# Graph attention and graph convolution on one core: products of 258 columns, the ones of the adjacency counted in the second layer, products ordered mask by mask, and a reordered first stage

## The reference

```python
h = jnp.maximum(_layernorm(x, axis=-1), 0.0)
# layer 0: graph attention, then a gated update
Wh = h @ W
src = Wh @ a[:F_out];  dst = Wh @ a[F_out:]
e = jax.nn.leaky_relu(src + dst.T, 0.2)
att = softmax(jnp.where(adj > 0, e, NEG_INF), axis=1)
h_prime = att @ Wh
gi = h_prime @ w_ih.T + b_ih;  gh = h @ w_hh.T + b_hh      # r, z, n as in a GRU cell
x = x + ((1.0 - z) * n + z * h)
# layer 1: graph convolution
h = jnp.maximum(_layernorm(x, axis=-1), 0.0)
x = x + adj @ (h @ W1.T + b1)
```

## Time and profile before

| | |
|---|---|
| median of 3 runs | 1602.78 us (1601.82 to 1603.23) |
| the profiled execution | 1601.98 us, of which the span is 1600.4 us |
| PE busy | 1534.7 us, 96% of the span |
| DVE busy | 1125.8 us, 70% |
| ACT busy | 1071.0 us, 67% |
| POOL busy | 40.5 us, 3% |
| DMA | 454.15 MB, mean 284 GB/s |

### The profile page before, as it was taken

The page is one execution under the profiler, slowest core; times in us unless marked ns, Lnnn a source line. Parts: engine busy times, 40 slices in busy tenths (PEclk is TensorE's granted clock), DMA queues, the critical chain, the costliest instruction groups (busy, mean ns, idle before and its releaser), DMA issues.

```text
span 1600.4 us, 34919 instructions
## 1 busy us (share of the span) xinstructions
PE 1534.7 (96%) x13260; PEld 1333.3 (83%) x13260; DVE 1125.8 (70%) x2274; ACT 1071.0 (67%) x1820; POOL 40.5 (3%) x59
## 2 busy tenths in 40 slices
PE   6369999999999999999999999999999999999998
PEld 5257888888888888888888888888888888888887
DVE  7898999999999999999999999999250000000001
ACT  6689999999999999999999999999121000000000
POOL 4000000000000000000000000000000000000000
PEclk9779999999999999999999999999999999999999
DMA  8759899999999999999999998997468444444430
GB/s 306 292 217 358 332 342 340 345 339 337 342 342 344 332 342 343 342 343 332 340 341 334 346 344 333 346 345 265 191 242 334 177 176 163 156 161 170 177 126 15
DMA packets 79954, 454.15 MB, mean 284 GB/s; under 512 B 9176, under 2 KB 38434, under 8 KB 58914
## 3 DMA queue, kind: packets, MB, share of 16 engines
q1 hardware_dynamic: 78322, 444.54, 74.9%
q10 hardware_dynamic: 1584, 8.98, 1.4%
HBM read 369.57 MB, written 83.92 MB: 283 GB/s over the span
## 4 chain that ended last, share of the span: by engine, by line
PE 93%; DVE 4%; ACT 1%; issue 1%; DMA 1%; SPq 0%; DVEq 0%
PE A L893 56%; PE A L975 28%; PE GP L917 3%; PE GP L918 2%; PE GQ L936 1%; PE GP L919 1%; PE GP L916 1%; ACT M L468 1%; DVE Y L618 1%; DVE JK L568 1%; DMA X<-in_adjb_dram 1%; DVE M L585 0%; PE TG L903 0%; PE TG L925 0%; DVE M L681 0%
## 5 line engine op out<-in xcount | busy, mean ns | idle before, releaser
L893 PE MATMUL A<-TB,M 128*128 128x259 f16 x8192 | 942.4, 275 | 37.8 <-DVE M L681 31.9
L893 PEld LDWEIGHTS A<-TB,M 128*128 128x128 fp8e4 x8192 | 798.2, 97 | 165.4 <-issue 39.0
L468 ACT ACTIVATE M<-SB,dsteep 128x256 fp8e4<-128x256 f32 x1180 | 484.5, 504 | 0.0
L477 ACT ACTIVATE JK<-X 128x4096 uint8<-128x4096 uint32 x124 | 448.4, 3616 | 0.0
L618 DVE TENSOR_SCALAR Y<-X 128x4096 fp8e4<-128x4096 f32 x128 | 293.1, 2290 | 9.9 <-DMA X<-in_adjb_dram 9.6
L796 DVE SCALAR_TENSOR_TENSOR hp<-A,R 128x256 f32<-128x256 f32 x32 | 13.6, 425 | 367.5 <-PE A L975 348.2
L669 DVE TENSOR_SCALAR M<-SB,nd 128x256 fp8e4<-128x256 f32 x868 | 238.4, 349 | 0.0
L975 PE MATMUL A<-WG,X 128*128 128x256 f16 x2048 | 225.7, 273 | 0.0
L975 PE MATMUL A<-WG,TB 128*128 128x256 f16 x2048 | 225.2, 273 | 0.0
L975 PEld LDWEIGHTS A<-WG,TB 128*128 128x128 fp8e4 x2048 | 200.4, 98 | 23.2
L975 PEld LDWEIGHTS A<-WG,X 128*128 128x128 fp8e4 x2048 | 200.4, 98 | 23.1
(11 more groups left out here) (132 smaller groups left out, 687.3 us busy)
## 6 DMA issues: line engine op xcount, KB each, us to landing
X<-in_adjb_dram SPq DMA_DIRECT2D x128, 2048.0 KB, 9.2
mask_bytes<-Y SPq DMA_DIRECT2D x128, 512.0 KB, 4.8
X<-mask_bytes SPq DMA_DIRECT2D x16, 2048.0 KB, 9.3
TB<-mask_bytes SPq DMA_DIRECT2D x16, 2048.0 KB, 9.2
M<-in_adjb_dram ACTq DMA_DIRECT2D x4, 2048.0 KB, 10.6
M<-in_xb_dram SPq DMA_DIRECT2D x8, 512.0 KB, 8.4
h_rows<-M SPq DMA_DIRECT2D x8, 512.0 KB, 3.6
R<-in_xb_dram SPq DMA_DIRECT2D x32, 128.0 KB, 6.7
```

The costliest lines, as they stand in the source:

```text
L468: ins = nc.scalar.activation(rows(mask1(c), jj), SB[u][:, :], ACT.Sigmoid, scale=STEEP, bias=dsteep[:, j:j + 1], saturate=False)
L477: nc.scalar.activation(junk, X[c % 2][:, :].bitcast(u32), ACT.Sign, accum_out=nz[:, bass.ts(g, 1), c:c + 1].rearrange("p g c -> p (g c)")) ...
L893: ins = nc.tensor.matmul(A[t][m][:, 0:2 * TW + 1], rows((mask1, mask2)[m](c), jj)[:, t * P:(t + 1) * P], TB[:, c * JC + jj, m, 0:2 * TW + ...
```

## The change

Five things change in the first program, besides the names of semaphores.

1. **258 columns.** The column of ones leaves the products: 2·TW = 258 columns. POOL's memset of the ones and DVE's small addition `cn` go. DVE's copy `den` goes too, because `rden` is now kept for all blocks.
2. **Ones counted in the second layer.** DVE's `halved(t)` adds the two halves of the fp8 bytes of block t (128 x 8192 each) into a buffer in the dead part of `TB`. ACT's `ones_sum(t)` sums that buffer (128 x 8192) into `cy`. Since both now read `YB[b]` or what is made of it, SP loads block t only after `finish(t-4)` (`q_o`), no longer after PE alone. `tally` and the two small products of the check move to the end.
3. **Mask by mask.** `products(g, c, m)` issues all 32 products of mask 1 of a chunk (two halves t of 16) and then all of mask 2. The first half waits only for mask 1 (`c_m1`). The banks are laid out so that ACT evacuates two banks with one instruction of 2 x 258 columns, and two feature banks likewise.
4. **First stage.** SP issues the load of the first `adj` chunk after column group 9, no longer after 11. DVE makes the first `Y` behind its constants, not ahead of them. In block 0 `table_high` of the third and fourth piece comes after 6 sign masks, no longer after 8.
5. POOL adds the epsilon (`ve`) that DVE added.

```diff
-                    if k in (11, 15):
-                        b = k // 4 - 2
+                    if k in (9, 15):
+                        b = k // 15
                         sp.dma_start(X[b][:, :], adjb[b, :, :]).then_inc(c_in[b], 16)
...
                     for b in range(4):
-                        sp.wait_ge(q_pe, k * 4 + b - 3)
+                        sp.wait_ge(q_o, k * 4 + b - 3)
                         y_load(k * 4 + b, b)
-                        sp.wait_ge(q_o, k * 4 + b - 3)
                         store(k * 4 + b - 4, b % 2)
...
-                        if isinstance(g, int) and g == 0 and jj == JC // 2:
+                        if isinstance(g, int) and g == 0 and jj == JC // 2 - 2:
                             for i in range(4 * c + 2, 4 * c + 4):
                                 table_high(i)
...
-                        for m in range(2):
-                            ins = nc.scalar.activation(AE[:, 2 * t + m, 0:2 * TW + 1], A[t][m][:, 0:2 * TW + 1], ACT.Copy)
-                        ins.then_inc(e_ev[t], 1)
+                        nc.scalar.activation(AE[:, 2 * m:2 * m + 2, 0:2 * TW], A3[m][:, :, 0:2 * TW], ACT.Copy).then_inc(
+                            e_ev[m], 1)
...
+                def ones_sum(t):
+                    act.wait_ge(q_half, 16 + t + 1)
+                    wait(act, q_sum, 16 + t)
+                    nc.scalar.activation(junk8, halves[t % 2], ACT.Copy, accum_out=cy[:, t:t + 1]).then_inc(q_sum, 1)
...
-                ones_of(0, 0, 0, 0)
-                dve.wait_ge(p_ev, 32)
+                dve.wait_ge(p_ev, 16)
...
+                ones_of(0, 0, 0, 0)
...
+                def halved(t, b, n):
...
+                    dve.wait_ge(q_in[b], (n + 1) * 16)
+                    if not isinstance(t, int) or t > 1:
+                        dve.wait_ge(q_sum, 16 + t - 1)
+                    dve.sem_inc(turn, 1)
+                    nc.vector.tensor_tensor(halves[b % 2], YB[b][:, 0:N], YB[b][:, N:2 * N], ALU.add,
+                                            saturate=False).then_inc(q_half, 1)
...
                 examine()
                 for b in range(4):
+                    halved(b, b, 0)
                     finish(b, b % 2, b, b // 2)
...
-                def products(g, c, t):
-                    for jj in range(JC):
-                        for m in range(2):
-                            ins = nc.tensor.matmul(A[t][m][:, 0:2 * TW + 1],
+                def products(g, c, m):
+                    for t in range(2):
+                        for jj in range(JC):
+                            ins = nc.tensor.matmul(A[t][m][:, 0:2 * TW],
```

More of the change, by code:

```diff
@@ L116, in binary_adjacency @@
         nz = sb("nz", [P, NS, CS])
-        cn = sb("cn", [P, NT])
-        den = sb("den", [P, NT])
+        cy = sb("cy", [P, NS])
         odd = sb("odd", [P, NS, 2])
@@ L136, in binary_adjacency @@
         Mf = M[:, :, :].rearrange("p c k -> p (c k)").bitcast(f32)
+        halves = [TBf[:, 16384 + b * N // 2:16384 + (b + 1) * N // 2].bitcast(f8) for b in range(2)]
+        junk8 = TBf[:, 16384 + N:16384 + 3 * N // 2].bitcast(u8)
         Z = [Mf[:, b * JC * RW:(b + 1) * JC * RW] for b in range(2)]
@@ L163, in binary_adjacency @@
         x1_d = nc.dram_tensor("x_after_gat", [P, NT, F], f32).ap()
-        A = [[ps(f"A{t}{m}") for m in range(2)] for t in range(2)]
+        ACC = ps("ACC", 4 * 512)
+        bank = [ACC[:, b * 512:(b + 1) * 512] for b in range(4)]
+        A = [[bank[2 * m + t] for m in range(2)] for t in range(2)]
+        A3 = [ACC[:, m * 1024:(m + 1) * 1024].rearrange("p (t f) -> p t f", f=512) for m in range(2)]
         TG = ps("TG")
@@ L194, in binary_adjacency @@
         g_in = [sem(f"g_in{b}") for b in range(2)]
-        e_t0, e_ev = sem("e_t0"), [sem(f"e_ev{t}") for t in range(2)]
+        e_m0, e_ev = sem("e_m0"), [sem(f"e_ev{m}") for m in range(2)]
         d_sum, d_n, d_rec, d_hp = sem("d_sum"), sem("d_n"), sem("d_rec"), sem("d_hp")
@@ L413, in features @@
                 def features(k):
[L414 to L420, removed]
+                    act.wait_ge(p_wh, k + 1)
+                    nc.scalar.activation(
+                        WG[:, k * 4:k * 4 + 4, 0:F + 2].rearrange("p (b t) f -> p b t f", t=2),
+                        A3[k % 2][:, :, 0:2 * (F + 2)].rearrange("p b (t f) -> p b t f", f=F + 2),
+                        ACT.Copy).then_inc(p_ev, 1)
                 act.wait_ge(p_one, 1)
@@ L481, in evacuate @@
                 def evacuate(q):
-                    for t in range(2):
-                        if t == 0:
-                            act.wait_ge(e_t0, q + 1)
+                    for m in range(2):
+                        if m == 0:
+                            act.wait_ge(e_m0, q + 1)
                         else:
@@ L561, in _ @@
                         act.dma_start(Z[n % 2], adjb[g * CS + c, :, :]).then_inc(c_in[n % 2], 16)
+                    ones_sum(n)
+                for t in range(LATE + 2, NS):
+                    ones_sum(t)
             @block.vector
@@ L842, in _ @@
                     for b in range(4):
+                        halved(k * 4 + b, b, k)
                         finish(k * 4 + b, b % 2, b, k * 2 + b // 2)
+                halved(NS - 4, 0, NS // 4 - 1)
+                for t in range(NS - 4, NS - 1):
+                    halved(t + 1, t % 4 + 1, NS // 4 - 1)
+                    finish(t, t % 2, t % 4, t // 2)
                 tally()
-                for t in range(NS - 4, NS):
-                    finish(t, t % 2, t % 4, t // 2)
-                    if t == NS - 3:
-                        judge()
+                judge()
+                finish(NS - 1, 1, 3, (NS - 1) // 2)
                 dve.wait_ge(k_all, 1)
@@ L956, in slot @@
                             pe.wait_ge(t_lo, 4 * (c + 1))
+                        for m in range(2):
+                            pe.wait_ge((c_m1, c_m2)[m], g * CS + c + 1)
                             if c == 0:
[L958 to L962 removed]
+                                wait(pe, e_ev[m], g)
                             pe.sem_inc(turn, 1)
[L964 to L965 removed]
+                            ins = products(g, c, m)
+                            if m == 1:
                                 ins.then_inc(c_pe, 1)
                             elif c == CS - 1:
[L968 removed]
+                                ins.then_inc(e_m0, 1)
                         after(g, u, k, c)
@@ L1010, in rest @@
                         ins = span(t, b, d, 0, NT)
+                        if d == 0 and isinstance(t, int) and t == NS - 1:
+                            sums()
                     ins.then_inc(q_pe, 1)
```

78 lines of the change are left out of this document (34 added, 44 removed).

## The result

The changed kernel takes 1606.53 us (median of 8 runs, 1604.38 to 1608.44), the kernel before 1602.63 us in the same comparison (8 runs, 1601.82 to 1604.93). The ratio is 1.0025, with an interval of 1.0014 to 1.0035: 0.25% slower, just more than can be told from no change. The profiled execution took 1607.55 us, its span 1606.1 us; against the 1601.98 us of before that is +5.6 us, where the prediction's sum said +7.4. The medians lie 3.9 us apart, so about 1.7 us of the 5.6 belong to these two executions and not to the change.

What follows compares the result with a forecast made beforehand. PE was taken to set the pace. Against 1601.98 us: -8.3 columns, +0.4 block 0, -0.1 first stage, +13.3 stall, +2.1 clock = 1609.4; with the median 0.8 above, 1610. Range 1600 up towards 1618.

Steps and rivals of the forecast that it cites:

- the columns: First layer, blocks 1 to 31: 258 columns instead of 259 take a product to 110.85 ns, 8.3 us gained.
- the stall: Second layer's start: load of row block 4 waits for `finish(0)` behind DVE's reductions and `halved(0)`; PE stands 13.3 us.
- rival A: First layer's products: the extra cost of 259 columns goes entirely, 110.0 ns each, 14.8 us gained, total 1603.7; chance 0.25.
- the order: First layer: changing bank and mask with each product was part of the extra cost, and ends with the new order.
- the row of 130 fp32 columns: First stage products, 260 cycles, 112 ns each, one bank, no mask change: taken to show an even number alone doesn't cure.
- Rival B: First layer: 258 columns cost as 259 do, nothing gained, sum +15.7, total 1618.5; chance 0.12 together with rival D.
- The landing: Second layer: the load of row block 4 takes 9.2 us from issue; longest 16.8 us.
- The clock: Second layer after PE's long wait: products run at the 1.2 GHz level for a while, 2.1 us added.
- First stage: Constants ahead of `Y` win about 2.0 us, stores delayed by the earlier load cost 1.8; taken as -0.1 us.
- block 0: First layer's first block: ACT's end of the chunk comes later through the moved `table_high`, +0.4 us once.
- No second stall: Second layer after row block 4: DVE needs 9.5 us a block against PE's 14.0, so it catches up.
- rival D: First layer gets bound by DVE or ACT, needing 1.1 us more a block; columns bring nothing; chance 0.12 together with Rival B.

Runs made afterwards that it cites:

- w258: The kernel before with products of 258 columns, old mask order, count of ones left out: 1595.24 us, ratio 0.9951.
- alt_t: The changed kernel with the two halves, and thus the PSUM banks, in turn within one mask: 1609.11 us in one run.
- al258: The kernel before with 258 columns, count of ones left out, and 264 columns of room per pair of tables: 1588.11 us in one run.
- w260: The kernel before with products of 260 columns, old mask order: 1602.52 us in one run.
- w257: The kernel before with products of 257 columns, old mask order, count of ones left out: 1595.85 us in one run.
- early_count_load: The changed kernel with ScalarE's second late 2 MB load of `adj` issued together with the first: 1604.27 us in one run.
- late_examine: The changed kernel with the check's two long reductions (`examine`) moved behind the second layer's first four finishes: 1588.19 us, ratio 0.9910 to the kernel before.
- runs259: The kernel before, still 259 columns, with 16 products of mask 1 and then 16 of mask 2 in each half: 1594.49 us, ratio 0.9945.
- al259: The kernel before with one constant changed, 264 columns kept for two tables instead of 260: 1594.24 us, ratio 0.9950.

## Why the prediction was right, and where it was not

The time came out where I had put it, 1606.5 for 1610, with the sign right. But two terms were mis-sized in opposite directions, the columns by 6.5 us and the stall by 2.6, so the agreement is partly luck: with the true price of the columns and all else as I had it, my sum was rival A's, 1603.7 us, and the forecast would have been no clear change.

- **The columns: mis-sized, -14.8 us instead of -8.3.** 110.85 ns for 258 columns was right for the columns alone (w258: 110.9). The step that failed is where rival A's second reason, the order, was set aside on the strength of the row of 130 fp32 columns. The order was worth another 0.9 ns (7936 x 0.9 = 7.1 us), through the table's place in memory and not through the bank or the mask (alt_t, al258). For the price rival A was right, 110.0 ns. (Two slips in its text change nothing in the sum: its low end, 1600.5, doesn't reach below the border of 1599.6, so a third of it had no place there; and by my own terms the border of 1606 is crossed at 110.3 ns, not at 110.1.)
- **Rival B and the coarser step.** Its argument, rounding up to a step, is true: 259 costs as 260 (w260). But the step is two columns (w257), so 258 lies below it, and B's price didn't occur.
- **The stall: mechanism right, 15.9 us instead of 13.3.** Place, cause and queue were as worked out: `halved` 8.68 us (8.6 taken), `finish(0)` from 1190.86, the load as releaser. The term that was mis-sized is the landing: 12.0 us for 9.2, the median of line L313, because of ScalarE's load beside it (early_count_load: 9.4). The same view had 16.8 as its longest; I didn't ask which transfer would run at the same time.
- **The clock: right**, 2.2 us for 2.1, at the level of 1.2 GHz (0.50) after the wait.
- **First stage and block 0: +2.1 us instead of +0.3, but the terms themselves were right.** Block 0 costs 0.36 us (0.4 taken). The constants win 1.6 to 2.1 us (2.0 taken) and the store behind the load costs 1.6 to 1.9 (1.8 taken). The profiled execution's column step at 41.70, 2.4 us later than before, looks like more, but 0.4 us of that are its later start. That start explains part of block 1's 124.17 us, too; late_examine and early_count_load have 123.37 and 123.42, against 123.31 before.
- **What I put at nothing: the clock at the start of block 1.** The first 64 products took 9.96 us instead of 8.76; the granted clock in 126 to 130 us was 0.52, against 0.96 before. All four executions with the changed kernel's first part have 9.96 to 10.10 us. The longer wait ahead of it (7.18 us instead of 5.92) isn't shown to be the cause: runs259 waits 6.33 us and takes 10.01, al259 waits 7.08 and takes 9.26, and w260, whose products cost what they cost before, waits 6.67 and takes 9.66. The cause stays open.
- **No second stall, no bound by DVE or ACT**: as forecast (rival D did not occur; 0.9 us of room were left).

Rival A's own sum was +0.9 us on the profiled execution of before, 1602.9. With the stall 2.6 us longer, the clock 0.1 and the start of block 1 1.8 us worse it becomes 1607.4, against the profiled 1607.55.

The Trainium skill, "TensorE: Matmul & The Clock Gate", Part 1, section "Wait — 56ns, not 53.3ns?" (N / 2.4 GHz plus about 2.5 ns) gives 110.0 ns for 258 columns, and the changed kernel agrees (110.0). It gives 110.4 for 259, where the kernel with tables 528 bytes apart (al259) and the one with 16 products of one mask in a row (runs259) show 110.9; the other 1.0 ns of the 111.9 goes with tables 520 bytes apart in turn. I had weighed the rule against the row of 259 columns, in which both effects were mixed, and that of 130 fp32 columns.

## What to carry to other kernels

When a price per instruction is a nanosecond off its neighbours, vary size, order and placement separately before attributing it: here an odd column and a distance of 520 bytes between tables were 7 to 8 us each, and the second goes with one constant. When a change adds a wait, ask what stands ahead of the awaited instruction on its engine and could stand behind it, and what other transfer runs beside the one that is awaited. Here a large load moved ahead on a queue held the small store behind it until it had landed itself, 8.2 us where the median of that line is 3.5. And before the difference of two single executions is put down to an edit, compare them at a point that the edit can't have reached: here they were 0.7 us apart by then.

## What the runs showed of the hardware

- Warm fp16 products by columns, stationary 128 x 128, from start to start: 110.0 ns (258), 110.9 (259) where successive tables lie 528 or 1040 bytes apart; 110.9 (257 and 258), 111.9 (259 and 260) where they lie 520 bytes apart in turn. 256 columns: 109.1 ns. Whether the distance or the alternating start counts is open.
- Alternating between two PSUM banks with each product costs nothing (alt_t and al258 against the changed kernel, all 14.08 us for 128).
- From the issue of a 2 MB load to PE's start it takes 9.4 us with no other large load issued beside it (one trace), and 12.0 to 12.1 us with another of 2 MB issued 0.9 us ahead on another queue (three traces).
- A DVE operation with two fp8 inputs takes 8.68 us over 8192 elements, as long as a reduction of 8192 fp16 elements (8.67): in these rows the one-byte type isn't faster than the two-byte one.
